# Rows of maxima carried to their place by DMA instead of TensorE and ScalarE, from the second chunk on

## What is computed

```python
x = x + xattn(layernorm(x), ctx, ctx, w_q, w_kv, w_concat)   # 16 heads of 16, one shared K and V, the 4096 keys of ctx
                                                             # (mem and kv are the same tensor, so the keys occur twice)
x = x + attn(layernorm(x), W_qkv, b_qkv, W_out, b_out)       # 16 heads of 64 over 256 tokens
x = x + ffn(layernorm(x), gate_w, gate_bias, Wg, Wu, Wd, Ws_g, Ws_u, Ws_d)   # 16 experts, 4 chosen, and a shared one
```

```python
qh = (q @ w_q) in 16 heads of 16;  k, v = ctx @ w_kv
prob = softmax(qh @ k.T / sqrt(16));  out = prob @ v
```

## Time and profile before

| | |
|---|---|
| median of three runs | 617.33 us (615.25 to 620.73) |
| the profiled execution, its own time | 613.31 us |
| its span | 611.5 us |
| TensorE matmul busy | 567.4 us, 93% of the span |
| VectorE busy | 458.6 us, 75% |
| ScalarE busy | 399.3 us, 65% |
| GpSimd busy | 121.9 us, 20% |
| mean granted TensorE clock | 0.988 |

### The profile page before, as it was taken

The page is one execution under the profiler, slowest core; times in us unless marked ns, Lnnn a source line. Parts: engine busy times, 40 slices in busy tenths (PEclk is TensorE's granted clock), DMA queues, the critical chain, the costliest instruction groups (busy, mean ns, idle before and its releaser), DMA issues.

```text
span 611.5 us, 11787 instructions
## 1 busy us (share of the span) xinstructions
PE 567.4 (93%) x4552; PEld 311.4 (51%) x4552; DVE 458.6 (75%) x668; ACT 399.3 (65%) x814; POOL 121.9 (20%) x158
## 2 busy tenths in 40 slices
PE   3788999999999999999999999898999986889996
PEld 1353344344344434434443443356766754878885
DVE  6696987988998999899899995416445657686555
ACT  1325877878888888888888888654546553345441
POOL 5000000000000000000000000312345453078763
PEclk9897999999999999999999999999999999999999
DMA  8963100001123000000000000100030010023301
GB/s 328 212 169 111 26 26 26 26 26 27 42 49 95 2 1 1 2 2 1 1 2 2 2 1 1 35 2 17 18 130 26 10 44 27 0 79 104 103 27 36
DMA packets 19483, 28.11 MB, mean 46 GB/s; under 512 B 5570, under 2 KB 13316, under 8 KB 18404
## 3 DMA queue, kind: packets, MB, share of 16 engines
q1 hardware_dynamic: 19428, 27.35, 15.6%
HBM read 20.78 MB, written 0.52 MB: 35 GB/s over the span
## 4 chain that ended last, share of the span: by engine, by line
PE 73%; DVE 19%; ACT 3%; issue 3%; DMA 1%; SPq 0%; DVEq 0%; ACTq 0%
PE bank L654 23%; PE bank L665 18%; DVE mxp L1224 11%; PE pairS L744 5%; PE pairS L908 4%; PE bank L926 3%; PE pairS L794 3%; PE pairS L673 2%; PE bank L821 2%; PE bank L908 2%; PE bank L807 2%; PE bank L597 2%; DMA ctx<-ctxT 1%; DVE Pb L1307 1%; ACT Pb L1022 1%
## 5 line engine op out<-in xcount | busy, mean ns | idle before, releaser
L1224 DVE TENSOR_REDUCE mxp<-pairS 128x1 f32<-128x1024 f32 x256 | 308.2, 1222 | 26.7 <-PE pairS L648 25.7
L1022 ACT ACTIVATE Pb<-bank 128x512 f32<-128x512 f32 x512 | 276.6, 598 | 57.5 <-PE bank L654 35.3
L654 PE MATMUL bank<-qparts,kparts 64*128 64x512 f32 x512 | 188.2, 454 | 7.7 <-DVE mxp L1224 4.2
L648 PE MATMUL pairS<-kparts,qparts 64*128 64x512 f32 x512 | 187.3, 456 | 4.5 <-DVE mxp L1224 3.3
L665 PE MATMUL bank<-Pb,V 128*32 128x256 f32 x2048 | 157.8, 391 | 1.2 <-ACT accS L1008 1.2
L654 PEld LDWEIGHTS bank<-qparts,kparts 64*128 64x128 f32 x512 | 77.4, 186 | 108.5 <-ACT Pb L1022 58.5
L665 PEld LDWEIGHTS bank<-Pb,V 128*32 128x32 f32 x2048 | 43.7, 108 | 84.0 <-issue 45.2
L648 PEld LDWEIGHTS pairS<-kparts,qparts 64*128 64x128 f32 x512 | 76.8, 186 | 11.2 <-DVE mxp L1224 5.4
L463 POOL CAST mparts<-mneg 128x8 fp32r<-128x8 f32 x16 | 3.1, 196 | 358.0 <-DVE mneg L1232 358.0
L478 POOL TENSOR_TENSOR Pb<-Pb,srd 128x512 f32<-128x512 f32 x32 | 33.3, 1039 | 64.8 <-DVE srd L1301 64.4
L1296 DVE TENSOR_REDUCE smx<-pairS 128x2 f32<-128x512 f32 x32 | 21.8, 686 | 31.6 <-PE pairS L794 31.6
(11 more groups left out here) (188 smaller groups left out, 712.6 us busy)
## 6 DMA issues: line engine op xcount, KB each, us to landing
ctx<-ctxT SPq DMA_DIRECT2D x4, 2048.0 KB, 10.0
wU<-w_up SPq DMA_DIRECT2D x18, 256.0 KB, 2.8
wD<-w_down SPq DMA_DIRECT2D x18, 128.0 KB, 2.1
wA<-w_qk SPq DMA_DIRECT2D x8, 256.0 KB, 2.6
qparts<-qh SPq DMA_DIRECT2D x120, 16.0 KB, 1.8
wO<-w_out SPq DMA_DIRECT2D x8, 128.0 KB, 2.1
kparts<-kvh SPq DMA_DIRECT2D x32, 32.0 KB, 2.0
wV<-w_v SPq DMA_DIRECT2D x2, 512.0 KB, 4.1
```

The source lines that it names most:

```text
L648: last = mm(dst[:, i * 512:(i + 1) * 512], qparts[rows, at:at + P], kparts[c // NCH][rows, k:k + 512], start=True, stop=True)
L654: mm(dst[:], kparts[g // NCH][rows, s * P:(s + 1) * P], qparts[rows, g * CW:(g + 1) * CW], start=True, stop=True).then_inc(exp_filled, 1)
L1022: A(PT[:, s % 8, :], src, ACT.Exp, scale=1.0 / np.sqrt(XD)).then_inc(exp_free, 1)
L1224: nc.vector.reduce_max(mxp[:, c % 2 * NBLK + blk, kp:kp + 1], pairS[n % 2][:], AX).then_inc(max_free, 1)
```

## The change

From the second chunk on, the rows of maxima no longer pass through TensorE, the ring of banks and ScalarE. The reduction and the split are made in two parts, blocks 0 to 2 when block 2's last pair is reduced (s = 14) and block 3 after s = 22. The split lands in `mcols`, a high and a low column for each block, and SyncE issues two DMAs for each block, one for the high and one for the low part: 128 pieces of four bytes, one from each partition, into 512 contiguous bytes of one row of `qparts`. The last chunk has them twice (rows 32, 33 and rows 96, 97), 16 DMAs instead of 8. Chunk 0 keeps the old way. The order on SyncE is rewritten: chunk c's eight row DMAs come first, then `place_q(c + 4)`; `place_k(0)` stands behind the rows of chunk 1 and `place_k(1)` behind those of chunk 3.

```diff
 LEAD = NBLK + 1
 SUMS_AT = 8
 NPAIR_K = S // 1024
+
+MAX_PARTS = range(0, NBLK - 1), range(NBLK - 1, NBLK)
 PRO = [("xT", 0), ("kv", 0, 0), ("qT", 0, 0), ("ks", 0, 0), ("ks", 0, 1), ("qs", 0), ("max", 0, 0, 0), ("max", 0, 1, 0),
        ("ks", 0, 2), ("ks", 0, 3), ("max", 0, 2, 0), ("max", 0, 3, 0), ("max", 0, 0, 1), ("kv", 0, 1), ("max", 0, 1, 1),
        ("max", 0, 2, 1), ("ks", 0, 4), ("ks", 0, 5), ("max", 0, 3, 1), ("max", 0, 0, 2), ("ks", 0, 6), ("ks", 0, 7),
...
 
 def placed():
 
-    at = {where: [what] for where, what in LATER.items()}
-    for g in range(1, NCHUNK):
-        at.setdefault((g - 1, 30), []).append(("rows", g))
-    return at
+    return {where: [what] for where, what in LATER.items()}
 
 
 BETWEEN = placed()
...
             V = [xb(f"V{b}", [P, KT, VW]) for b in range(B)]
             mxp = xb("mxp", [P, 2 * NBLK, NPAIR_K])
             mneg = xb("mneg", [P, 2, NBLK])
-            mparts = [xb(f"mparts{i}", [P, NBLK, 98], F32R) for i in range(2)]
+            mparts = xb("mparts", [P, NBLK, 34], F32R)
+            mcols = [xb(f"mcols{i}", [P, 2, NBLK], F32R) for i in range(2)]
             accS = xb("accS", [P, 512])
             oden = xb("oden", [P, NBLK])
         kTb = [sb(f"kTb{i}", [P, B * L]) for i in range(3)]
...
         max_filled, max_free = sem("max_filled"), sem("max_free")
         low_done, pick_done = sem("low_done"), sem("pick_done")
         plain_done, plain_in = sem("plain_done"), sem("plain_in")
-        ks_in, qs_in = ([sem(f"{n}_in{i}") for i in range(2)] for n in ("ks", "qs"))
+        ks_in, qs_in, rows_in = ([sem(f"{n}_in{i}") for i in range(2)] for n in ("ks", "qs", "rows"))
         mneg_ready, dve_const = sem("mneg_ready"), sem("dve_const")
         wA_in, wV_in = ([sem(f"{n}_in{i}") for i in range(2)] for n in ("wA", "wV"))
         wO_in = [sem(f"wO_in{i}") for i in range(3)]
...
                                          part[32 * j:32 * j + XD, s, :].bitcast(F32)
                                          ).then_inc(ks_in[s], 16)
 
+            def place_rows(c, part):
+
+                sp.wait_ge(mparts_ready, 2 * c + 1 + part)
+                for r in (32, 96)[:2 if c == NCHUNK - 1 else 1]:
+                    for blk in MAX_PARTS[part]:
+                        at = c * CW + blk * P
+                        for n in range(2):
+                            sp.dma_start(qparts[r + n:r + n + 1, at:at + P].bitcast(F32),
+                                         mcols[c % 2][:, n, blk:blk + 1].bitcast(F32)).then_inc(rows_in[c % 2], 16)
+
             def q_parts(m, b):
                 sp.wait_ge(exp_free, EXP_TURN["qT", m, b] + 1)
                 sp.wait_ge(low_done, HALVED.index(("qT", m, b)) + 1)
...
             sp.dma_start(gb[:], gate_b.rearrange("(o n) -> o n", o=1).broadcast_to([P, E])
                          ).then_inc(late_in, 16)
             q_parts(1, 0)
-            for c in range(4, 8):
-                place_q(c)
-            q_parts(1, 1)
-            for c in range(8, NCHUNK):
-                place_q(c)
-            for s in range(2):
-                place_k(s)
+            sp.wait_ge(plain_in, 64)
+            for c in range(1, NCHUNK):
+                if c == 1:
+                    place_q(4)
+                for part in range(2):
+                    place_rows(c, part)
+                if c == 1:
+                    place_k(0)
+                if c == 3:
+                    place_k(1)
+                    q_parts(1, 1)
+                if c + 4 < NCHUNK:
+                    place_q(c + 4)
             for g in range(2):
                 load(wV[g], w_v, g, wV_in[g])
 
...
             ch.step(nc.gpsimd.memset(accS[0:64, :], 0.0))
             nc.gpsimd.memset(accS[32:34, :], 1.0).then_inc(plain_done, 1)
             pool.wait_ge(plain_done, 1)
-            for m in mparts:
-                ins = nc.gpsimd.memset(m[:].bitcast(F32), 0.0)
-            ch.step(ins)
+            ch.step(nc.gpsimd.memset(mparts[:].bitcast(F32), 0.0))
             ch.step(nc.gpsimd.memset(one_row[:], 1.0))
             nc.gpsimd.memset(cw[:, :, 0:2], 1.0).then_inc(const_done, 1)
             for c in range(NCHUNK):
-                hi, lo = mparts[c % 2][:, :, 32:98:64], mparts[c % 2][:, :, 33:98:64]
-                least = mneg[:, c % 2, :].unsqueeze(2).broadcast_to([P, NBLK, 2])
-                pool.wait_ge(mneg_ready, c + 1)
-                if c >= 2:
-                    pool.wait_ge(exp_filled, EXP_TURN["rows", c - 2] + 1)
-                ch.step(CP(hi, least))
-                TT(lo, least, hi.bitcast(F32), ALU.subtract).then_inc(mparts_ready, 1)
+                for part, blocks in enumerate(MAX_PARTS):
+                    of = slice(blocks.start, blocks.stop)
+                    hi, lo = (mcols[c % 2][:, n, of] if c else mparts[:, of, 32 + n] for n in range(2))
+                    least = mneg[:, c % 2, of]
+                    pool.wait_ge(mneg_ready, 2 * c + 1 + part)
+                    if c > 2 and part == 0:
+                        pool.wait_ge(rows_in[c % 2], 128 * ((c - 1) // 2))
+                    ch.step(CP(hi, least))
+                    TT(lo, least, hi.bitcast(F32), ALU.subtract).then_inc(mparts_ready, 1)
 
 
             def low_proj(p):
...
 
                 if what[0] == "ks":
                     landed, n = ks_in[what[2] // 4], 24
+                elif what[0] == "rows":
+                    landed, n = rows_in[what[1] % 2], 8 * ((what[1] + 1) // 2) + (8 if what[1] == NCHUNK - 1 else 0)
                 else:
                     landed, n = qs_in[what[1] % 2], 12 * ((what[1] + 1) // 2)
                 if not placed_already:
...
 
             def max_rows(c):
                 dst = exp_bank(("rows", c))
-                pe.wait_ge(mparts_ready, c + 1)
+                pe.wait_ge(mparts_ready, 2)
                 for i in range(NBLK):
-                    last = mm(dst[0:98, i * P:(i + 1) * P], mparts[c % 2][:, i, :], identr[:], start=True, stop=True)
+                    last = mm(dst[0:34, i * P:(i + 1) * P], mparts[:, i, :], identr[:], start=True, stop=True)
                 last.then_inc(exp_filled, 1)
 
             turn_of = {"xT": x_T, "qT": q_T, "kv": kv_proj, "ks": k_rows, "v": v_rows_of, "qs": q_rows,
...
 
             def max_move(c):
                 src = filled(("rows", c))
-                if c == NCHUNK - 1:
-                    A(qparts[96:98, c * CW:(c + 1) * CW], src[96:98, :], ACT.Copy)
                 A(qparts[32:34, c * CW:(c + 1) * CW], src[32:34, :], ACT.Copy).then_inc(exp_free, 1)
 
             move_of = {"xT": x_move, "qT": q_high, "kv": kv_high, "ks": k_move_rows, "v": v_move_rows,
...
                 n = MAX_TURN["max", c, blk, kp]
                 dve.wait_ge(max_filled, n + 1)
                 nc.vector.reduce_max(mxp[:, c % 2 * NBLK + blk, kp:kp + 1], pairS[n % 2][:], AX).then_inc(max_free, 1)
-                if (blk, kp) == (NBLK - 1, NPAIR_K - 1):
-                    block_max(c, n)
-
-            def block_max(c, n):
+                if kp == NPAIR_K - 1:
+                    for part, blocks in enumerate(MAX_PARTS):
+                        if blk == blocks[-1]:
+                            block_max(c, n, part, blocks)
+
+            def block_max(c, n, part, blocks):
                 dve.wait_ge(max_free, n + 1)
                 if c >= 2:
-                    dve.wait_ge(mparts_ready, c - 1)
-                nc.vector.tensor_reduce(out=mneg[:, c % 2, :], in_=mxp[:, c % 2 * NBLK:(c % 2 + 1) * NBLK, :],
+                    dve.wait_ge(mparts_ready, 2 * (c - 2) + 1 + part)
+                at = c % 2 * NBLK
+                nc.vector.tensor_reduce(out=mneg[:, c % 2, blocks.start:blocks.stop],
+                                        in_=mxp[:, at + blocks.start:at + blocks.stop, :],
                                         op=ALU.max, axis=AX, negate=True).then_inc(mneg_ready, 1)
 
             def sums_rows(g, src, done):
```

## The result

The kernel after takes 642.68 us, the median of four runs (640.18 to 646.13). The kernel before took 617.35 (615.25 to 620.73) on the same chip. The ratio is 1.042, with a 95% interval of 1.036 to 1.049. The forecast was 632 with a range of 622 to 648: slower, as forecast, by 25.3 us instead of 15.1. The profiled execution of after is the slowest of the four, 646.13 us with a span of 644.3, so its own difference from the earlier trace rows is 32.8 us. Some executions of any of these kernels run at a lower granted clock and take longer; every ratio in this document leaves out those more than 1.5% above the fastest of their kernel.

What follows compares the result with a forecast made beforehand. TensorE was taken to bound the kernel, VectorE almost in step. Chunk 2 +9.0, chunk 3 -0.5, chunk 4 +5.6, chunks 5 to 14 -4.9, chunk 15 +1.7, clock three times +1.4: +15.1 on 617.3, 632 us, range 622 to 648.

Steps and rivals of the forecast that it cites:

- The gains: TensorE's transposing matmuls removed: 0.49 us a chunk in chunks 1 to 14, 1.3 in chunk 15, 8.2 us in all.
- What was costed at nothing: Second reduction on VectorE, second split on GpSimd and wV's later load, all hidden: 0 us.
- Issue and landing: SyncE's row DMAs: 0.63 us per issue, 1.8 us from issue to landing.
- Chunk 1: place_q(4) ends at 68.82: SyncE's queue at chunk 1: eight row DMAs start only at 68.82, making step 0 3.0 us late.
- 9.0 us later than before in all: Step 0 of chunk 2, behind place_k(0) and place_q(5) in SyncE's queue: 9.0 us late, including chunk 1's delay.
- 5.6 us more: Step 0 of chunk 4, 36 copies ahead of its rows: 28.2 us after chunk 3's instead of 22.6.
- I take 1.4, since TensorE is dense after the wait: Lower clock behind the waits of chunks 2, 4 and 15: 1.4 us each, 4.2 together.
- my upper bound of 4.2: Most that the lower clock could cost TensorE after one wait: 4.2 us, for ten microseconds at that level.
- The queue is in time: Rival: SyncE issues in under 0.53 us, the waits vanish and only the gain is left; 609 us, 5%.
- Four-byte pieces are slow: Rival: a row DMA takes 1.0 us to issue (651 us) or 3.1 to land (640 us); 14%.
- The clock stays: Rival: row DMAs issue in 0.5 us, waits are short and the clock doesn't fall; 623 us, 12%.

Runs made afterwards that it cites:

- the kernel of eighteen: The change with place_q(4) behind chunk 1's rows, at most 18 copies between two chunks' rows, last chunk's rows by block: 611.12 us, ratio 0.988.
- GpSimd's queue: The change with row DMAs issued by GpSimd, SyncE's copies in the order of before, last chunk's rows by block: 611.66 us, ratio 0.988.
- the kernel of eighteen with its last chunk in two: The kernel of eighteen with the last chunk's 16 row DMAs in two parts, as in the change: 620.15 us, ratio 0.995.
- the one with the delays: The kernel of eighteen with 3 to 12 idle copies ahead of the last two row DMAs of chunks 5, 7, 9, 11, 13: 634.56 us, ratio 1.026.
- that of the two parts alone: The kernel before with only the maxima's reduction and split made in two parts: 620.73 us, ratio 1.003.
- the first two experiments: The change with place_q(4) behind chunk 1's rows: 647.5 us; the change with place_k spread over chunks 1 to 6 and place_q's lead shortened: 627.33 us.

## Why the forecast was right in kind and short in size

- **The gains: right.** The period of an ordinary chunk fell by 0.50 us (0.49 forecast); in the kernel of eighteen the whole gain is 8.4 us in medians (8.2 forecast). That they agree so well is partly luck: the interval goes from 4.6 to 10.5 us, and the two profiled executions lie only 4.5 us apart; that of the kernel of eighteen lost 1.7 us to the low stretch of its chunk 15 and 0.8 to its two waits.
- **What was costed at nothing: right.** The second reduction and split left the period at 21.55 us. wV, now issued at 398.08, landed by 403.5, and VectorE first read it at 418.96.
- **Issue and landing: nearly right.** The row DMAs ran at 0.64 (10.19 us for 16) instead of 0.63, and landed in 2.0 instead of 1.8. In chunk 4 one issue took 1.45 us, so the eight took 5.95. Not forecast is the late landing in chunk 6: I had said that the waits would stand at four chunks and at no other.
- **"Chunk 1: place_q(4) ends at 68.82": short by 1.8 us.** In after the rows start at 70.65. place_q(4) begins 1.45 us later than in before, and its copies took a little longer. Everything in the queue up to chunk 2 comes later by that, so "9.0 us later than before in all" became 11.5: 1.8 from the start, 0.4 from the eight slower rows of chunk 1, 0.2 from the landing.
- **Chunk 4, "5.6 us more": 6.6.** Step 0 came 29.24 us after that of chunk 3, for 28.2 forecast; most of the difference is the slow issue among its rows (1.45 us). Chunk 3 itself was 1.7 us later than the shift of chunk 2 (0.9 forecast), which is the clock's 2.1 less 0.49.
- **"I take 1.4, since TensorE is dense after the wait": the step that failed in size.** Behind the waits of chunks 1, 2 and 4 the clock cost 1.7, 2.1 and 2.1 us (behind chunk 2: 132.62 - 106.67 = 25.95, where before had 24.29 with the 0.49 still in it). In chunk 15 it cost 6.3, above my upper bound of 4.2, since the clock stayed at the lower level for 16 us where I had allowed 10 at most. This one term is 4.9 of the 10.7 us by which the forecast was short in the profile. The sum to the first matmul of the next stage was forecast as 15.1 and is 25.8 in the profile: 2.5 for chunk 2, 0.7 for the clock after it, 1.1 for chunk 4, 1.5 from there to chunk 15 (0.7 of it the clock behind chunk 4, 0.4 the wait of chunk 6, 0.3 chunk 15), 4.9 for the last.
- **The rivals.** "The queue is in time" would have given 609. It is what GpSimd's queue and the order of eighteen reach, 611.7 and 611.1, and it was wrong for the order of the change, since an issue took 0.63 and not under 0.53 us. "Four-byte pieces are slow" is out: 1.9 to 2.0 us to landing in the median, and of the ordinary chunks only chunk 6 waits. "The clock stays" is out: every wait of 2.5 us or more had a stretch at 1.2 GHz in it or behind it. The converse doesn't hold: in chunk 15 of two kernels, and in chunk 3 of a third (0.66 in the mean from 127 to 132 in the kernel of eighteen with its last chunk in two), the clock fell without such a wait.

Not settled: the profile of after has 7 us more behind the cross-attention (from its first matmul to the end of the span 214.9 us for 207.8), and it goes with the clock: the mean granted clock of that stretch is 1.00 in before and 0.95 in after. Over all kernels the two go together: 207.8 to 207.9 us at 1.00 (before, the kernel of eighteen and the one with the delays), 210.3 to 211.1 at 0.97 or 0.98 (five kernels with and without a wait in chunk 15, one of them that of the two parts alone, which has no row DMAs), 214.9 to 215.2 at 0.95 (after and the kernels of the first two experiments). So up to 3 us of it come without the change, and what brings the rest isn't shown. Nor do the medians settle it. 19.5 us up to chunk 15 and 6.3 in it make 25.8, close to the 25.3 between the medians, but these 25.8 are of the slowest execution of after, 3.5 us above its median, and of one of before that lies 4.0 us below; the executions in between have no trace.

## What to carry to other kernels

Before a small transfer that something waits for is put on a queue, count the issues that stand ahead of it between the moment its data is ready and its due time, chunk by chunk, at the measured pitch (0.63 to 0.68 us here): a queue that was busy some 60% of the stretch (320 issues of 0.64 us in 336) hid two places with 36 copies in a row, and spreading the same copies to at most 18, with the last chunk's rows sent block by block, turned a loss of 4% into a gain of 1.2%. Or give the deadline its own issuing engine, one that is idle in that stage. And price a wait of TensorE at more than its length once it is as long as those behind which the clock was seen to fall (2.5 us here; 1.1 us cost only itself), with a wide range where TensorE's work is less even, as in chunk 15.

## What the runs showed of the chip that I had not expected

- 128 pieces of four bytes, from 128 partitions into one row, land in 2.0 us when issued by SyncE and 1.9 by GpSimd, about as long as the 16-row copies of 1.8; single ones took over 3. The number of packets below 512 bytes rose by 18,432.
- An issue costs GpSimd 0.545 us and SyncE 0.63 (2.48 us for four and a gap). GpSimd paused once for 2.60 us behind an issue, in chunk 15 of both kernels that issue there, and the profile doesn't show why.
- A wait of 1.09 us left the clock at 2.4 GHz; waits of 2.5 to 6.8 us brought 1.2 GHz for a stretch worth 1.5 to 2.2 us in dense chunks. In chunk 15, with TensorE busy for 4.9 and 5.0 of 5 us in two windows of after, the clock stayed down for 16 us behind a wait of 3.3, in the kernel of GpSimd's queue for 3.7 us behind one of 5.2, and in the kernel of eighteen for 3.4 us behind none that was longer than 0.43.
